# Graph attention layers on Trainium2: attention work started a slot earlier, the skip connection as an accumulating DMA

## The reference

```python
h = maximum(layernorm(x), 0)
mask = adj + eye(n) > 0
for l in range(3):
    si, sj = h @ attn_w[l, :d], h @ attn_w[l, d:]
    scores = leaky(si[:, :, None] + sj[:, None, :] + attn_b[l])      # slope 0.2
    attn = softmax(where(mask, scores, -inf))
    agg = einsum('bij,bjd->bid', attn, h)
    g = layernorm(h + agg) * g1[l] + beta1[l]
    ff = gelu(g @ W1[l] + b1[l]) @ W2[l] + b2[l]                     # 256 -> 1024 -> 256
    h = layernorm(g + ff) * g2[l] + beta2[l]
return x + h
```

## Time and profile before

| | before |
|---|---|
| median of 3 runs | 2631.7 us (2631.31 to 2631.83) |
| the profiled execution | 2632.32 us |
| its span, first to last instruction | 2630.5 us |
| PE busy | 2283.2 us, 87% |
| DVE busy | 1775.0 us, 67% |
| ACT busy | 1887.8 us, 72% |
| POOL busy | 1904.6 us, 72% |
| moved by DMA | 121.12 MB, mean 46 GB/s |
| mean granted clock of TensorE | 0.993 |

### The profile page before, as it was taken

One profiled execution on the slowest core, in us unless ns is written; L12 is line 12 of the kernel. 1 busy time (PEld: TensorE's weight loads), 2 busy tenths in 40 slices (PEclk: granted clock), 3 DMA queues, 4 the chain that ended last, 5 costly groups with the idle time before them and its releaser, 6 DMA issues.

```text
span 2630.5 us, 46306 instructions
## 1 busy us (share of the span) xinstructions
PE 2283.2 (87%) x15840; PEld 1555.4 (59%) x15840; DVE 1775.0 (67%) x5890; ACT 1887.8 (72%) x3498; POOL 1904.6 (72%) x1639
## 2 busy tenths in 40 slices
PE   2889999998888999998888999999888889999997
PEld 1566666665555666665555666666555566666665
DVE  5676666666776666766767676666677676666664
ACT  3777777767767777777677777776776777777774
POOL 2477777677787767777777777777778777767787
PEclk9899999999999999999999999999999999999999
DMA  5221111112232010112223111110223211011222
GB/s 158 73 57 47 23 25 17 25 33 67 75 101 49 17 25 17 25 21 53 73 77 77 41 25 21 21 25 17 57 73 101 53 17 25 17 25 17 41 55 74
DMA packets 280170, 121.12 MB, mean 46 GB/s; under 512 B 209792, under 2 KB 278400, under 8 KB 279936
## 3 DMA queue, kind: packets, MB, share of 16 engines
q1 hardware_dynamic: 279936, 118.15, 19.3%
HBM read 51.01 MB, written 16.78 MB: 26 GB/s over the span
## 4 chain that ended last, share of the span: by engine, by line
POOL 33%; ACT 31%; DVE 19%; issue 9%; PE 6%; DMA 1%; SPq 0%; POOLq 0%; DVEq 0%
POOL rstd L787 7%; ACT norm L494 6%; POOL X L833 6%; POOL X L831 6%; POOL norm L817 6%; POOL X_lo L809 5%; ACT probs L519 5%; ACT L484 5%; ACT L519 5%; ACT p_hid L484 4%; ACT g_hi L489 4%; DVE g_lo L577 4%; DVE scores L639 4%; DVE row_top L645 2%; DVE bn L584 2%
## 5 line engine op out<-in xcount | busy, mean ns | idle before, releaser
L577 DVE TENSOR_TENSOR g_lo<-p_hid,g_hi 128x512 f16<-128x512 f32 x768 | 527.8, 687 | 677.9 <-ACT g_hi L489 673.7
L401 PE MATMUL p_pair<-w_hi,g_hi 128*128 128x256 f16 x3072 | 837.8, 273 | 0.0
L401 PE MATMUL p_pair<-w_lo,g_hi 128*128 128x256 f16 x3072 | 837.6, 273 | 0.0
L401 PE MATMUL p_pair<-w_hi,g_lo 128*128 128x256 f16 x3072 | 837.4, 273 | 0.0
L484 ACT ACTIVATE p_hid<-p_hid,b_eff 128x512 f32<-128x512 f32 x768 | 504.5, 657 | 217.9 <-PE p_hid L387 216.7
L387 PE MATMUL p_hid<-hT_hi,w_hi 128*128 128x512 f16 x1536 | 458.7, 380 | 178.2 <-DVE g_lo L577 178.0
L494 ACT ACTIVATE norm<-res,shift,rstd 128x256 f32<-128x256 f32 x384 | 199.2, 589 | 409.5 <-POOL shift L789 409.5
L489 ACT ACTIVATE g_hi<-p_hid 128x512 f16<-128x512 f32 x768 | 458.5, 597 | 24.4
L387 PE MATMUL p_hid<-hT_lo,w_hi 128*128 128x512 f16 x1536 | 458.4, 380 | 0.2 <-DMA hT_lo<-h_lo 0.2
L387 PE MATMUL p_hid<-hT_hi,w_lo 128*128 128x512 f16 x1536 | 458.6, 380 | 0.0
L805 POOL TENSOR_TENSOR h_lo<-norm,h_hi 128x1024 f16<-128x1024 f32 x96 | 204.8, 2133 | 344.6 <-ACT h_hi L539 344.6
(11 more groups left out here) (67 smaller groups left out, 3662.1 us busy)
## 6 DMA issues: line engine op xcount, KB each, us to landing
x_in<-in_x SPq DMA_DIRECT2D x32, 512.0 KB, 3.8
w_f<-in_x SPq DMA_DIRECT2D x32, 512.0 KB, 5.7
out<-w_f SPq DMA_DIRECT2D x32, 512.0 KB, 5.0
adj_in<-in_adj SPq DMA_DIRECT2D x32, 256.0 KB, 4.4
w_f<-in_L_gnn_W SPq DMA_DIRECT2D x6, 1024.0 KB, 6.9
hT_hi<-h_hi SPq DMA_TRANSPOSE x96, 3.1
hT_lo<-h_lo SPq DMA_TRANSPOSE x96, 3.1
attn_rows<-in_L_gnn_attn_w SPq DMA_DIRECT2D x1, 768.0 KB, 6.6
```

The costliest lines, as they stand in the source:

```text
L401: mm = pe.matmul(ff_banks(s)[:, t, :], g[i][:, nodes], w[l][:, c, :], start=(c == 0 and t % 2 == 0 and n == 0), stop=(c == C - 1 and n == ...
L577: dve.tensor_tensor(g_lo[i][:], p_hid[k][:], g_hi[i][:], ALU.subtract).then_inc(g_lo_ready, 1)
```

## The change

It makes two things different.

**The attention starts a slot earlier.** FIRST_SLOT is -6. Dot products are made for item s+4 (DVE, step 5), the spreading of s_j (PE, step 3), the scores and maxima (DVE, step 4) and the exponentials (ACT, step 5) for item s+3, one item further ahead than before. The transposes of the probabilities (PE), pT_hi (ACT), pT_lo and the reciprocal (DVE) stay at item s+2 but move to step 4, and the aggregation is for item s+2 at step 6, where it was for s+1 at step 0. Input statistics are for s+6, the input norm for s+5. s_j is now spread into the other pair of banks, so `transpose_probs` waits for `res2_ready` and the aggregation waits for the scores of the next item. On POOL the inverse deviation of the attention norm comes first in the slot. The feed-forward statistics move from step 4 to step 3. The ring stays at eight groups.

**The skip connection is a DMA.** SP no longer loads x a second time. POOL, instead of adding, issues a DMA that reads x from memory and adds it to `y_out` in SBUF; SP's store waits for its landing. It follows DVE's output for the last item too, and x_steps then counts four for every item.

```diff
@@ -51,10 +51,10 @@
 LAG = 3
-FIRST_SLOT = -5
+FIRST_SLOT = -6
...
 LOOPS = ITEMS // PER - 1
-FOLD_AT = {0: 0, 2: 1, 4: 2}
+FOLD_AT = {0: 0, 3: 1, 5: 2}
...
 def layer_of(s):

@@ -92,8 +92,7 @@
 
-    v = 4 * s + RING * (s // PER) + max(0, s % PER - (PER - RING)) + n
-    return (4 * PER + RING) * r + v if isinstance(r, int) else r * (4 * PER + RING) + v
+    return 4 * (PER * r + s) + n
...
 def group_of(r, s):

@@ -174,7 +173,6 @@
         y_out = [w1_f32[:, i, :].rearrange("p (t d) -> p t d", t=T) for i in range(2)]
-        x_again = [w2_f32[:, i * T:(i + 1) * T, :] for i in range(2)]
...
 

@@ -224,8 +222,9 @@
 
+
         def sj_bank(s):
-            return agg_banks(s)[:, 0:2, :].rearrange("p a (u n) -> p (a u) n", n=N)
+            return p_pair[s % 2][:, 0:2, :].rearrange("p a (u n) -> p (a u) n", n=N)
...
             return agg_banks(s)[:, 2:4, :].rearrange("p a (u n) -> p (a u) n", n=N)

@@ -239,7 +238,7 @@
         adj_loaded = [sem(f"adj_loaded{i}") for i in range(2)]
-        x_again_loaded = [sem(f"x_again_loaded{i}") for i in range(2)]
+        skipped = [sem(f"skipped{i}") for i in range(2)]
...
         x0_ready = sem("x0_ready")

@@ -308,15 +307,10 @@
 
-            def load_again(g):
-                sp.dma_start(x_again[g % 2], graphs(x, g)).then_inc(x_again_loaded[g % 2], 16)
-
...
                 g = group_of(r, s)
-                sp.wait_ge(x_steps, x_total(r, s, 5))
+                sp.wait_ge(skipped[g % 2], 16 * (g // 2 + 1))
                 sp.dma_start(graphs(out, g), y_out[g % 2]).then_inc(stored[g % 2], 16)
-                if g + 2 < G:
-                    load_again(g + 2)
...
                 i = s % 2

@@ -328,9 +322,9 @@
             def slot(r, s):
-                if is_item(r, s + 3) and layer_of(s + 3) == 0 and group_of(r, s + 3) + 2 < G:
-                    sp.wait_ge(x0_ready, group_total(r, s + 3, 4, 4))
-                    load_x(group_of(r, s + 3) + 2)
+                if is_item(r, s + 4) and layer_of(s + 4) == 0 and group_of(r, s + 4) + 2 < G:
+                    sp.wait_ge(x0_ready, group_total(r, s + 4, 4, 4))
+                    load_x(group_of(r, s + 4) + 2)
...
                     load_adj(group_of(r, s + 3) + 2)

@@ -346,10 +340,6 @@
                     weights((s + 3) // 2, 1)
-                if (r, s) == (0, 5):
-                    sp.wait_ge(w_lo_ready, 4 * L)
-                    load_again(0)
-                    load_again(1)
...
             load_adj(0)

@@ -416,8 +406,8 @@
                 pe.wait_ge(dots_ready, total(r, s, 8, 8))
-                if later(r, s, 3):
-                    pe.wait_ge(res2_ready, total(r, s - 3, 2, 2))
+                if later(r, s, 4):
+                    pe.wait_ge(res2_ready, total(r, s - 4, 2, 2))
...
                     pe.wait_ge(bias_ready, FOLD_AT[s] + 1)

@@ -427,6 +417,8 @@
                 pe.wait_ge(probs_ready, total(r, s, 4, 4))
+                if later(r, s, 3):
+                    pe.wait_ge(res2_ready, total(r, s - 3, 2, 2))
...
                 mm.then_inc(pT_psum, 1)

@@ -435,6 +427,8 @@
                 pe.wait_ge(X_lo_ready, total(r, s, 1, 1))
+                if is_item(r, s + 1):
+                    pe.wait_ge(score_steps, total(r, s + 1, 5, 4))
...
                 for t in range(T):

@@ -451,17 +445,17 @@
                         hidden(r, s, c)
-                    if c == 7 and is_item(r, s + 2):
+                    if c == 4 and is_item(r, s + 2):
...
 
-                    if c == 3 and is_item(r, s + 2):
-                        spread_sj(r, s + 2)
-                    if c == 0 and is_item(r, s + 1):
-                        aggregate(r, s + 1)
+                    if c == 3 and is_item(r, s + 3):
+                        spread_sj(r, s + 3)
+                    if c == 6 and is_item(r, s + 2):
+                        aggregate(r, s + 2)
...
             slots(pe, slot)

@@ -553,11 +547,11 @@
                     if c == 4 and is_item(r, s + 2):
-                        exponentials(r, s + 2)
-                    if c == 6 and is_item(r, s + 2):
                         copy_probs(r, s + 2)
-                    if c == 7 and is_item(r, s + 4) and layer_of(s + 4) == 0:
-                        norm_input(r, s + 4)
+                    if c == 5 and is_item(r, s + 3):
+                        exponentials(r, s + 3)
+                    if c == 7 and is_item(r, s + 5) and layer_of(s + 5) == 0:
+                        norm_input(r, s + 5)
...
 

@@ -689,7 +683,6 @@
                 dve.wait_ge(stored[s % 2], 16 * (G // 2 - 1))
-                dve.wait_ge(x_again_loaded[s % 2], 16 * G // 2)
...
                     g2_pair, beta2_pair = (v[:, L - 1, :].unsqueeze(1).broadcast_to([P, 2, D])

@@ -698,14 +691,12 @@
                     dve.tensor_tensor(y[:, pair, :], y[:, pair, :], beta2_pair, ALU.add).then_inc(x_steps, 1)
-                dve.wait_ge(x_steps, x_total(r, s, 4))
-                dve.tensor_tensor(y, y, x_again[s % 2], ALU.add).then_inc(x_steps, 1)
...
             def slot(r, s):
-                starts = is_item(r, s + 5) and layer_of(s + 5) == 0
-
-                late = isinstance(r, int) and (r, s) == (0, -4)
-                if isinstance(r, int) and (r, s) == (0, -3):
+                starts = is_item(r, s + 6) and layer_of(s + 6) == 0
+
+                late = isinstance(r, int) and (r, s) == (0, -5)
+                if isinstance(r, int) and (r, s) == (0, -4):
...
                     dve.tensor_scalar(g1_scale[:], g1_col[:], WSCALE, None, ALU.mult).then_inc(scale_ready, 1)

@@ -716,8 +707,8 @@
                     if c == 2 and starts and not late:
-                        dve.wait_ge(stat_steps[0], group_total(r, s + 5, 10, 4))
-                    if isinstance(r, int) and (r, s, c) == (0, -3, 1):
+                        dve.wait_ge(stat_steps[0], group_total(r, s + 6, 10, 4))
+                    if isinstance(r, int) and (r, s, c) == (0, -4, 1):
...
                         hidden(r, s, c)

@@ -725,31 +716,30 @@
                         feed_residual(r, s - 1)
-                    if isinstance(r, int) and (r, s, c) == (0, -3, 0):
+                    if isinstance(r, int) and (r, s, c) == (0, -4, 0):
                         input_statistics(0, 1)
-                    if isinstance(r, int) and (r, s, c) == (0, -3, 1):
+                    if isinstance(r, int) and (r, s, c) == (0, -4, 1):
...
                     if c == 1 and starts and not late:
-                        input_statistics(r, s + 5)
+                        input_statistics(r, s + 6)
                     if c == 2 and starts and not late:
-                        aggregates(0, group_total(r, s + 5, 10, 8))
-                    if c == 3 and isinstance(r, int) and r == 0 and s + 2 in FOLD_AT:
-                        add_bias(FOLD_AT[s + 2], sj_bank(s + 2))
-                    if c == 3 and is_item(r, s + 2):
-                        add_scores(r, s + 2)
-                        row_maxima(r, s + 2)
-                    if c == 4 and is_item(r, s - 1):
+                        aggregates(0, group_total(r, s + 6, 10, 8))
+                    if c == 3 and is_item(r, s - 1):
                         feed_statistics(r, s - 1)
+                    if c == 4 and is_item(r, s + 2):
+                        low_probs(r, s + 2)
+                        row_sums(r, s + 2)
+                    if c == 3 and isinstance(r, int) and r == 0 and s + 3 in FOLD_AT:
+                        add_bias(FOLD_AT[s + 3], sj_bank(s + 3))
+                    if c == 4 and is_item(r, s + 3):
+                        add_scores(r, s + 3)
+                        row_maxima(r, s + 3)
...
                         aggregates(2, total(r, s - 1, 10, 8))
-                    if c == 4 and is_item(r, s + 3):
-
-                        dot_products(r, s + 3, 0)
-                        dot_products(r, s + 3, 1)
-                    if c == 6 and is_item(r, s + 2):
-                        low_probs(r, s + 2)
-                    if c == 6 and is_item(r, s + 2):
-                        row_sums(r, s + 2)
+                    if c == 5 and is_item(r, s + 4):
+
+                        dot_products(r, s + 4, 0)
+                        dot_products(r, s + 4, 1)
...
                     if c == 7 and is_item(r, s + 2):

@@ -836,22 +826,23 @@
                 pool.wait_ge(x_steps, x_total(r, s, 4))
-                pool.wait_ge(x_again_loaded[i], lane_total(r, s - 2 * RING))
-                pool.tensor_tensor(y_out[i], y_out[i], x_again[i], ALU.add).then_inc(x_steps, 1)
+                g = group_of(r, s)
+                pool.dma_start(y_out[i], x.rearrange("(g t) n d -> n g t d", t=T)[:, g],
+                               accum_op=ALU.add).then_inc(skipped[i], 16)
...
                     pool.wait_ge(res_rows_ready, 1)
+                if is_item(r, s + 1):
+                    inverse_deviation(s + 1, 1, total(r, s + 1, 10, 10), total(r, s + 1, 2, 1))
...
                     low_X(r, s + 2)
```

(9 more changed lines are left out.)

## The result

The changed kernel takes 2336.95 us (median of 4 runs, 2334.1 to 2338.3) against 2631.76 us (4 runs, 2631.31 to 2632.63): a ratio of 0.8878, 95% interval 0.8863 to 0.8893. 294.8 us are gone. The forecast was 2344. The profiled execution took 2337.64 us with a span of 2335.8; TensorE's mean granted clock was 0.993, as before, so its clock has no part in the result.

A forecast was written before the change was run, and what follows sets the result against it. A ring over POOL, ACT and DVE bounds before, PE after. Span 2630.5 less 282.6 (90 intervals) and 16 (first slots), plus 7 and 4.5 (start, end), is 2343.4; with 1.2 over the span, 2344.6 us; range 2310 to 2436.

The forecast's parts named there:

- The ring that set the pace: Waits around POOL, ACT and DVE, with ACT's norm behind POOL's layer output and X_lo, set 25.56 us a slot.
- fifth rival: Some wait takes over the full 2.5 us in regular slots; only long slots gain, 94 us, 2537; chance 0.03.
- PE's floor: PE's hidden and feed matmuls, aggregation and transposes sum to 23.0 us in every slot, the bound of regular slots after.
- The next ring: From one attention shift to the next over ACT, DVE and POOL: 22.6 us in regular slots, 0.4 under PE.
- Long slots: Slots where POOL also takes an input norm's rstd and shift: 28.49 us before, 23.6 expected after.
- second rival: A ring over ACT, DVE and POOL stays longest, with DVE's mask add contending with POOL: 2436 us; chance 0.20.
- the sum: Regular slots of 23.1 and long ones of 23.6 us, weighted 16 and 8 of 24, give 23.27 an interval.
- The skip connection: POOL's 2.36 us add becomes a DMA, hidden from SP and PE: nothing in steady state.
- third rival: The DMA's issue holds POOL 2.9 us beyond its spare time in 31 long slots: +90, 2434 us; chance 0.12.
- The fourth: Rival: the adding transfer lands late and PE lacks hidden input, a loss from about 36 us landing; about 2780; chance 0.05.
- Start and end: Item 0 comes 7 us later, the first five slots gain 16 us, the last DMA adds 4.5 us.
- Added waits: PE: spread_sj waits for res2, charged up to 0.5 us in long slots; aggregation's wait for scores hidden with 2.5 to spare.

The follow-up runs named there:

- both experiments that open this ring alone: `x_pool_order`, and the kernel before with only POOL's order changed, the attention norm's inverse deviation first in the slot: 2361.57 us.
- x_pool_order: The changed kernel with POOL's old order, the attention norm's inverse deviation behind layer output, X_lo and input norm: 2514.07 us, ratio 0.9549.
- x_pe_cut: The changed kernel without the feed's product of g_hi and w2_lo, less work for PE: 2309.58 us, ratio 0.8772.
- x_no_skip: The changed kernel with the skip connection left out, neither DMA nor addition: 2321.86 us, ratio 0.8820.
- x_pool_pad: The changed kernel with one more product on POOL in each slot from slot 4, behind h_residual: 2421.56 us, ratio 0.9191.
- x_mask_free: The changed kernel with DVE's input statistics at step 2, their aggregate at step 3 and the mask moved from step 6 to step 2: 2365.88 us.
- x_mask_early: The changed kernel with DVE's mask making moved from step 6 to step 5: 2340.53 us, ratio 0.8892.
- b_dma_skip: The kernel before with only the skip connection changed to POOL's accumulating DMA: 2640.50 us, ratio 1.0020.
- x_pool_add: The changed kernel with POOL's addition and SP's second load of x again instead of the DMA: 2347.37 us, ratio 0.8918.

## Why the prediction was right, and where its steps were not

**The ring that set the pace: right.** It named POOL's shift behind layer output and X_lo, and both experiments that open this ring alone end it in regular slots. What it didn't say is that there each of the two edits opens it alone: it summed the new order and the earlier aggregation as one. Its fifth rival, in which only long slots gain, fell with the first row of after; nearest to it is `x_pool_order`, and there it is the regular slots that gain.

**PE's floor: right.** 23.0 summed, 23.02 measured, and `x_pe_cut` shows that PE holds it. The next ring was put at 22.6 and is 22.42. It was 0.2 too long, which decided nothing here.

**Long slots: the term that was mis-sized.** Taken 23.6 from bounds of 23.1 to 23.7; measured 24.03 in five of eight and 23.93 in the mean of the eight (25.40, 22.88, 23.00, 24.04, 24.02, 24.03, 24.03, 24.02 in the first change of ring). The bound itself was good: without contention, in `x_no_skip`, they take 23.35. What failed is the step that kept contention out of the sum, with the argument that at that step "POOL should be in short instructions of 0.5 us". It is in L789, of 2.35 us. Contention costs 0.7 a slot, a third of the 2.1 that the second rival allowed. "2.8 of a 23.0 slot are spare" for POOL was too much for the same slots: 1.97 of 24.03 are idle, and by `x_pool_pad` 3.6 us are to be had in regular slots, while in long ones 3.3 of them show.

**How often, and the luck in the sum.** The sum weighed long slots with 8 of 24, some 30 of the 89 intervals. Only three of the four rounds have another behind them: 24 of 89, in both kernels. The mean interval was put at 23.27 and is 23.19, the 90 intervals at 2091.8 and are 2083.5. That they are so near is partly luck, since two misses cancel. The 24 long ones cost 8.6 us more than put (23.96 in the mean against 23.6). The other 65 are 22.90 in the mean, not 23.1, 12.9 us less, because of the 21.8 and 22.4 in each round. The wrong count takes off 2.8 more, the last interval 1.0.

**The skip connection: mechanism partly right.** Hidden from SP and PE, yes: SP waits for the landing 50.4 us in 11 cases, but only 7.0 of them between 200 and 2280 us, and PE's waits for a transpose in that part are 0.3 us, those of its weight loads 2.6. Not "nothing in steady state": 10.5 us, since POOL's work, which the issue and the two slower instructions lengthen by 1.9 us, lies in the ring of a long slot. The bounds of its issue, 0 to 5.7 us, hold the 0.88 measured, and with the slower instructions 1.9. The landing was 5.8 us, as the plain load's 5.7 had it. The figures of the Trainium skill, DMA: Bandwidth & Descriptors, "Anatomy of one DMA", give 3.2 us by estimate and were too short for this transfer: measured 5.8. By them the sum would have changed by 2.5 us, not 2. The third rival, an issue that holds POOL beyond its spare time, named the right term at 90 us, against the 10.5 measured. The fourth, slower, needed a landing of 36 us.

**Start and end: right.** Item 0 came 6.3 us later (+7 put), the first five slots took 133.8 us (133), the last interval 19.77 (20.8), and behind item 95's h_lo it was 5.7 us more (+4.5). For the start the cause was the named one. The timeline of DVE in the kernel after:

```profile
46.54 1.40 DVE L578 BATCH_NORM_STATS2 bn<-x_in 128x6 f32<-128x256 f32 x4 [3.88 <-DMA x_in<-in_x]
...
48.53 0.68 DVE L662 TENSOR_TENSOR pT_lo<-p_pair,pT_hi 128x512 f16<-128x512 f32 x1
```

Item 0's pT_lo stands behind statistics that wait 3.88 us for their load; 51 was put, 48.5 measured. Item 0's aggregation then begins at 50.46, released by item 1's scores, the wait that the change added.

**Added waits: right.** The aggregation's wait for the scores doesn't occur behind the start, and spread_sj's for `res2` is 13.3 us in 18 cases, against 14.3 in 25.

**What stays open.** The first of the eight long slots takes 25.3 us, the one behind the eight 21.8, and two intervals a round 22.4; in `x_no_skip` they take 24.3, 22.1 and 22.4 to 22.6. Which wait ends last there wasn't tried.

## What to carry to other kernels

Where every engine runs an order of its own, follow the ring of waits once round before adding a stage: here two small instructions moved ahead of long ones on POOL bring 92% of the whole gain by themselves (271.5 of 294.8); the stage more and the DMA share the remainder. Test a bound by taking work off the engine: if the slots stay, it wasn't the bound. Test idle time by putting work in, and then look at the rows beside it: here the added work lengthened another engine's row. Look for rows that are longer than their like, and count the engine that lengthens them into the ring, though no wait names it.

## What the runs showed of the hardware

- The add for the mask on DVE (128x1024, two inputs) took 0.68 us alone, and where it began during a long POOL instruction it ended 0.5 to 0.6 us after that: 1.14, 1.38, 1.78 and 2.22 us.
- The DVE instruction behind it, with one tensor as input (128x512, int32 to bf16), took 0.43 us alone and 1.38 (`x_mask_free`), 2.47 (`x_mask_early`) and 3.71 us (`x_pool_pad`) beside long POOL instructions; each time it ended 0.3 us after POOL's. POOL's small rstd was lengthened too: 1.02 to 1.49, behind L789, while DVE's add was under way.
- Issuing an accumulating DMA of 512 KB takes a row of 1.34 us on POOL, of which the next instruction overlaps all but 0.88, and lands after 5.8 us. The two POOL instructions right behind it ran 0.5 us longer each (2.13 to 2.63, 2.36 to 2.85). In `b_dma_skip`, where h_lo begins 4.3 us after the start of the issue, it takes its 2.12; in `x_pool_add`, with the same order and no DMA, both have their usual 2.13 and 2.35.
- The added POOL product of 128x2048 elements, which reads the same rows as both inputs, took 3.60 us, not twice the 2.36 of one of 128x1024; beside DVE's mask row it took 4.05.
